# The rotary sine product on GpSimd, from a ScalarE copy of the projected query, in a two-layer attention and expert kernel

## What is computed

```python
def _apply_rope(x, sin, cos):
    return x * cos + _rotate_half(x) * sin
q_hk = (hidden_q @ Wq.T).reshape(Bv, Sv, H, K)
q_big = jnp.einsum('bshk,hkq->bshq', q_hk, w_kc_q)
q_big = _apply_rope(q_big, sin_q[None, :, None, :], cos_q[None, :, None, :])
q_r = jnp.einsum('bshq,hqr->bhsr', q_big, W_qr)
k_r = jnp.einsum('bld,hdr->bhlr', kv_r, W_kr)
scores = jnp.einsum('bhsr,bhlr->bhsl', q_r, k_r)
attn = jax.nn.softmax(scores, axis=-1)
```

## Time and profile before

| | |
|---|---|
| median of three runs | 660.13 us |
| the profiled execution, first to last instruction | 657.1 us |
| TensorE busy | 545.1 us (83%) |
| VectorE busy | 439.8 us (67%) |
| GpSimd busy | 307.2 us (47%) |
| ScalarE busy | 260.9 us (40%) |
| mean granted TensorE clock | 0.942 of full speed |
| batch 0, 1, 2, 3 begin at | about 114, 240, 371, 503 us |

### The profile page before, as it was taken

How to read it: one execution, slowest core, us unless ns; L and a number is a source line. 1 busy time by engine, 2 the same in 40 slices (tenths; PEclk the granted TensorE clock), 3 DMA queues, 4 the chain that set the end, 5 groups by cost and what they waited for, 6 DMA issues and landing times.

```text
span 657.1 us, 8656 instructions
## 1 busy us (share of the span) xinstructions
PE 545.1 (83%) x3032; PEld 341.7 (52%) x3032; DVE 439.8 (67%) x874; ACT 260.9 (40%) x706; POOL 307.2 (47%) x300
## 2 busy tenths in 40 slices
PE   2862865857898779789998897999987999999696
PEld 1851334535553457555555575555554765655442
DVE  3999893479757725997776459977774364644244
ACT  1852221243532333545345234453452165464243
POOL 3766344249628642336154442361544234445366
PEclk9986699898987799999999998999999899999798
DMA  7940100022312200000000000000000000000000
GB/s 289 399 150 6 59 0 4 1 65 96 97 33 96 88 1 21 0 5 1 1 0 1 0 17 1 1 1 1 0 2 0 17 1 1 0 2 1 17 0 16
DMA packets 10201, 24.56 MB, mean 37 GB/s; under 512 B 4464, under 2 KB 6512, under 8 KB 9264
## 3 DMA queue, kind: packets, MB, share of 16 engines
q1 hardware_dynamic: 9920, 23.24, 10.0%
q0 software_dynamic: 240, 0.79, 0.3%
HBM read 22.97 MB, written 1.05 MB: 37 GB/s over the span
## 4 chain that ended last, share of the span: by engine, by line
PE 45%; DVE 35%; ACT 7%; issue 6%; POOL 6%; DMA 0%; SPq 0%; POOLq 0%; DVEq 0%; ACTq 0%
PE s L515 9%; PE qc L515 9%; PE ga L515 9%; PE qb L515 8%; PE ua L515 6%; DVE wk L1070 4%; DVE top L1068 4%; ACT reg L865 3%; DVE reg L1154 3%; DVE amax L995 2%; PE tp L518 2%; DVE nmax L1161 2%; DVE masks L1232 2%; DVE ffn L1014 2%; DVE reg L1127 2%
## 5 line engine op out<-in xcount | busy, mean ns | idle before, releaser
L1399 POOL TENSOR_TENSOR reg<-reg,rsum 128x512 f32<-128x512 f32 x64 | 68.4, 1089 | 131.9 <-DVE rsum L1168 131.9
L865 ACT ACTIVATE reg<-s,nmax 128x256 f32<-128x256 f32 x128 | 59.0, 477 | 49.8 <-DVE nmax L1161 49.7
L1232 DVE SCALAR_TENSOR_TENSOR masks<-s,route,masks 128x256 f32<-128x256 f32 x120 | 51.4, 478 | 38.3 <-PE s L515 38.0
L515 PE MATMUL s<-wE,xhi 128*128 128x512 fp8e4 x192 | 74.4, 387 | 0.6
L515 PE MATMUL s<-wE,xlo 128*128 128x512 fp8e4 x192 | 74.2, 387 | 0.0
L515 PE MATMUL qc<-reg,wM 128*64 128x256 f32 (+1 forms) x384 | 69.6, 402 | 3.0 <-DVE reg L1154 3.0
L518 PE MATMUL tp<-idn,reg 128*128 128x128 f32 x248 | 40.4, 286 | 35.5 <-POOL reg L1399 19.0
L515 PE MATMUL qb<-reg,wA_hi 128*128 128x256 f16 x384 | 65.0, 279 | 1.5 <-ACT reg L847 1.4
L518 PEld LDWEIGHTS tp<-idn,reg 128*128 128x128 f32 x248 | 29.5, 144 | 50.7 <-POOL reg L1399 25.6
L515 PEld LDWEIGHTS qc<-reg,wM 128*64 128x64 f32 (+1 forms) x384 | 37.5, 155 | 31.9 <-issue 22.2
L783 ACT COPY reg<-tp 128x512 f32<-128x512 f32 x52 | 30.6, 588 | 56.5 <-PE tp L518 56.5
(11 more groups left out here) (194 smaller groups left out, 1118.4 us busy)
## 6 DMA issues: line engine op xcount, KB each, us to landing
masks<-in_moe_masks SPq DMA_DIRECT2D x16, 512.0 KB, 3.3
wM<-in_att_wq SPq DMA_DIRECT2D x1, 2048.0 KB, 7.9
wE<-in_wo_t SPq DMA_DIRECT2D x1, 2048.0 KB, 10.7
reg<-in_kc_q SPq DMA_DIRECT2D x1, 1536.0 KB, 11.2
reg<-in_qr_t SPq DMA_DIRECT2D x1, 1536.0 KB, 18.6
xb<-in_x SPq DMA_DIRECT2D x4, 256.0 KB, 3.4
wU<-in_gate_w SPq DMA_DIRECT2D x1, 1024.0 KB, 13.1
wD<-in_up_w SPq DMA_DIRECT2D x1, 1024.0 KB, 15.1
```

The source lines that it names most:

```text
L515: return nc.tensor.matmul(dst, lhsT, rhs, start=start, stop=stop, skip_group_check=not check)
L865: nc.scalar.activation(attn[p % 2][:, k * S:(k + 1) * S], s.tensor[:, (k % 2) * S:(k % 2 + 1) * S], ACT.Exp, bias=nmax[:, o:o + 1], accum_ ...
L1232: ins = nc.vector.scalar_tensor_tensor(acc[:, t, chain], src, w, acc[:, t, chain], ALU.mult, ALU.add)
L1399: nc.gpsimd.tensor_tensor(a, a, rsum[:, o + 2 * hh:o + 2 * hh + 2].unsqueeze(2).to_broadcast([P, 2, S]), ALU.mult).then_inc(attn_ready.sem, 1)
```

## The change

The sine product leaves VectorE. ScalarE copies the projected 128x768 tile from QB into a new SBUF tile `qcopy`, and GpSimd multiplies that by the sine table into the second half of `qcs`. VectorE keeps the cosine product, which reads QB as before, and which now also waits for the copy. `to_keys` on TensorE also waits for the sine product. The copies stand on ScalarE at these places: pair 0 after `x_turn` and ahead of the adjacency drain, pair 1 after `to_keys` of pair 0 and ahead of the tanh of the adjacency, pair p + 2 in slot p after the expert fills of the second group and ahead of `attn_turn`. The products stand on GpSimd: pair 0 as the first thing of a batch, pair 1 after `adjacency`, pair p + 2 after `attention` of slot p. For the SBUF that `qcopy` takes, the scratch space of dynamic DMAs is halved to 8192.

```diff
+        qcopy = sb("qcopy", J * S)
...
-        qc_ready = count("qc_ready", PAIRS)
+        q_copied = count("q_copied", PAIRS)
+        sin_ready = count("sin_ready", PAIRS)
...
             def to_keys(b, p):
                 pe.wait_ge(QB.drained, QB.done(("project", b, p)))
+                pe.wait_ge(sin_ready.sem, sin_ready.at(b, p + 1))
...
+            def rotate(b, p):
+
+                act.wait_ge(QB.filled, QB.done(("project", b, p)))
+                act.wait_ge(sin_ready.sem, sin_ready.at(b, p))
+                nc.scalar.copy(qcopy[:, :], QB.tensor[:, 0:J * S]).then_inc(q_copied.sem, 1)
...
                 x_turn(b)
+                rotate(b, 0)
                 if more:
                     adjacency(b + 1)
                 to_keys(b, 0)
+                rotate(b, 1)
                 if more:
                     adjacency_tanh(b + 1)
                     norm(b + 1, 0, y2, xb, y2_ready)
...
                     experts_of(experts[p][1])
+                    if p + 2 < PAIRS:
+                        rotate(b, p + 2)
                     attn_turn(b, p, 0)
...
-                for g, tab in enumerate((cosq, sinq)):
-                    nc.vector.tensor_tensor(qcs[:, g * J * S:(g + 1) * J * S], QB.tensor[:, 0:J * S], tab[:, :],
-                                            ALU.mult).then_inc(qc_ready.sem if g == 0 else QB.drained, 1)
+                dve.wait_ge(q_copied.sem, q_copied.at(b, p + 1))
+                nc.vector.tensor_tensor(qcs[:, 0:J * S], QB.tensor[:, 0:J * S], cosq[:, :], ALU.mult).then_inc(QB.drained, 1)
...
+            def rotate(b, p):
+
+                if p == 0:
+                    pool.wait_ge(ld_tab.sem, 112)
+                pool.wait_ge(q_copied.sem, q_copied.at(b, p + 1))
+                if p >= 1:
+                    pool.wait_ge(QC.filled, QC.done(("to_keys", b, p - 1)))
+                nc.gpsimd.tensor_tensor(qcs[:, J * S:2 * J * S], qcopy[:, :], sinq[:, :], ALU.mult).then_inc(sin_ready.sem, 1)
...
                 more = b + 1 < B
+                rotate(b, 0)
                 if more:
                     adjacency(b + 1)
+                rotate(b, 1)
                 if b >= 1:
                     rstd(b - 1, 3)
                 for p in range(PAIRS):
                     attention(b, p)
+                    if p + 2 < PAIRS:
+                        rotate(b, p + 2)
...
-    nc = _bacc.Bacc("TRN2", target_bir_lowering=False, num_devices=1)
+    nc = _bacc.Bacc("TRN2", target_bir_lowering=False, num_devices=1, dynamic_dma_scratch_size=8192)
```

## The result

The changed kernel takes 689.98 us, the median of four runs (687.24 to 692.93), against 659.42 us for the kernel before beside it: 4.7% more, ratio 1.0473, 95% interval 1.044 to 1.0507. The forecast was 686, with a range of 667 to 695. The profiled execution has a span of 685.4 us, 28.3 more than the 657.1 of before.

A forecast was written before the change was run, and what follows sets the result against it. TensorE, busy 83%, was taken as the bound, with VectorE time worth something only where a matmul waits for it. The terms sum to 25.7 us: span 657.1 becomes 682.8, plus 3.0 for the median, 686 us; range 667 to 695.

The forecast's parts named there:

- Term 1: Batch 0, pair 1: to_keys starts 5.4 us later behind copy, tanh and adjacency; 3.6 us plus 1.7 clock, 5.3 us.
- Term 2: Batch 0, attention of pair 1 to pair 3: two sines enter a nearly full GpSimd; 3.0 us, ends 0 and 4.5.
- Terms 3 and 4: Starts of batches 2 and 3: sine behind result and store on GpSimd delays to_keys; 5.7 and 4.6 us with clock.
- Term 5: Five slots of batches 1 to 3: copy behind ScalarE's expert fill makes VectorE late; 1.3 us x 5 = 6.5 us.
- Term 6: Slot 0 of batches 1 to 3, copy wait and disturbed subtraction; slot 5 of batches 1 and 2, late sine; 3.0 us.
- Term 7: Gain in slots 1 and 2 of batches 1 and 2, bounded by TensorE's own waits; 2.4 us won.
- Its signs: TensorE waits of some 6, 4 and 6.5 us, cosine waits over 2 us in five slots, GpSimd gapless in batch 0.
- Rival (c): Full blocking: each sine holds up VectorE's two-input instructions for its whole 1.8 us; 692 us; chance 0.13 with dearer cases.
- rival (a): Moved work pays: the chain's 10 us come in; 659 us, or 650 with TensorE slack at two batch starts; chance 0.07.

The follow-up runs named there:

- pair1_ahead: Changed kernel with the copy of pair 1 behind the adjacency tanh and its sine between the GpSimd addition and the rstd; 685.28 us, ratio 1.038.
- scratch_alone: Kernel before with only the scratch of dynamic DMAs halved; 659.08 us, ratio 0.999.
- b0_back: Changed kernel with all eight sine products of batch 0 back on VectorE; 679.65 us, ratio 1.0312.
- five_products: Changed kernel with only five of 32 sines on GpSimd and the copy ahead of the second group; 652.94 us, ratio 0.9923 to the kernel before.
- p2_back: Changed kernel with the sine product of pair 2 back on VectorE in batches 1 to 3; 689.64 us, ratio 1.047.

## Why the prediction was right, step by step

The sign, the mechanism and the size held; the sum was 25.7 us and 28.3 were measured in the trace. Part of the agreement is luck: terms 3 to 6 were short by 5.5 us together, and terms 1, 2 and 7 and the end of the kernel, which no term had, made up 3.0 of them. By its terms, each from the steps of the shift:

```
                                          predicted  measured
1  batch 0, pair 1                            5.3       5.0
2  batch 0, GpSimd full                       3.0       1.9
3  start of batch 2                           5.7       6.65
4  start of batch 3                           4.6       5.28
5  five slots, copy behind an expert fill     6.5       8.8
6  slot 0 (3.3) and slot 5 (1.3) *            3.0       4.6
7  won                                       -2.4      -2.9
   behind the last pair                        -       -1.1
                                             25.7      28.3

* slot 5's late sine is that of pair 7; it shows from pair 6 to pair 7
```

**Its signs.** The waits of TensorE are 6.30, 4.02 and 6.68 us where some 6, 4 and 6.5 were named, and the cosine waits 3.71 or 3.72 us for the copy in each of the five slots of term 5. One sign wasn't met: GpSimd isn't busy without a gap from `attention` 1 to 3, since 1.3 us stay idle, 0.87 of it in one wait for a mask.

**Prices.** 0.80 and 1.8 us were read off neighbouring shapes; 0.799 and 1.817 are measured. Taking the copy by the step from 256 to 512 columns, and the product between the two rows that bound it, was enough.

**Term 1** held as worked out: 5.18 us later, and one low-clock stretch behind it. `pair1_ahead` shows the cause. The windows view of the changed kernel, from that `to_keys` on, has the clock at 0.50, and the same after the waits of 4.02 and 6.68 us:

```profile
134.40:137.70 3.30, 3.30 (x10) 1.91 (x12) 0.18 (x1) 1.07 (x6) 1.87 (x2) 0.50 0.00 0
...
390.29:397.11 6.82, 5.50 (x20) 3.13 (x21) 0.68 (x2) 0.73 (x2) 1.22 (x1) 0.50 0.11 37
...
530.23:537.06 6.83, 4.65 (x16) 2.53 (x17) 0.00 (x0) 0.62 (x2) 2.06 (x2) 0.50 0.11 38
```

**Terms 3 and 4.** The waits were worked out at 4.0 and 4.65 us and came to 4.10 and 4.70: the order on GpSimd could be read to a tenth. What was mis-sized is the clock. In batch 2 it was put at one stretch of 3.41 us, 1.7 us lost; the stretch is 6.82 us long and costs 6.65 - 4.10 = 2.6 us, since part of it is TensorE's own wait. In batch 3, which paid some already, 0.6 us more. The bounds of term 3 (4.0 to 5.7) didn't hold the 6.65.

**Term 2** is mis-sized, or given back. The stretch is 25.11 us long with 23.83 busy, against 22.11 and 20.36 in the earlier trace rows: 3.0 us more, to the digit of the forecast. The windows view of the changed kernel:

```profile
151.82:176.93 25.11, 18.90 (x112) 12.77 (x112) 18.22 (x50) 9.95 (x29) 23.83 (x25) 0.81 0.28 91
```

But from pair 1 the shift grows by 4.07 us to pair 4, falls by 2.28 from there to pair 6, and 1.9 are left at the start of batch 1. The forecast stopped its reading at `attention` 3 and didn't ask what comes behind. What gave the time back lies at least in part in the trace of the kernel before. It has a low stretch there, which `scratch_alone`, the same streams, hasn't. Before, then `scratch_alone`:

```profile
202.59:209.41 6.82, 5.67 (x7) 2.50 (x8) 5.13 (x8) 0.60 (x1) 5.89 (x5) 0.50 0.47 154
```

```profile
202.59:209.41 6.82, 6.71 (x31) 3.87 (x32) 5.97 (x10) 1.81 (x4) 5.80 (x6) 1.00 0.47 155
```

The shift of `scratch_alone` falls by 4.4 us from pair 4 to pair 6, and that of `b0_back`, with the batch 0 of the kernel before, does so too. The changed kernel has the full clock from 183 to 212 us. So the 1.9 us measured for this term are a difference between two clock patterns as well, and its worth without them stays open.

**Term 5** was right in its five slots and short in size: 2.29, 2.22, 2.00, 1.15 and 1.15 us, not 1.3 each. The one slot that was read closely (slot 4, batch 3) is one of the two with 1.15. The other three were priced by it without a reading of their own. In slot 1 of batch 3, VectorE had 0.97 us to spare ahead of its masks, not 1.20, and hadn't waited for the bank before; its masks start 2.0 us later, and that is the cost. In slot 3 of batches 1 and 2 a second thing comes in. VectorE in batch 1, from its masks on, before:

```profile
299.30 1.74 DVE L1232 SCALAR_TENSOR_TENSOR masks<-s,route,masks 128x256 f32<-128x256 f32 x4 [1.21 <-PE s L515]
...
301.66 0.18 DVE L1000 TENSOR_SCALAR qsc<-amax 128x16 f32<-128x16 f32 x1
...
302.16 0.69 DVE L1005 TENSOR_TENSOR ffn<-ffn,qrs 128x512 f32<-128x512 f32 x1
```

and after, with GpSimd beside it:

```profile
307.08 1.65 DVE L1244 SCALAR_TENSOR_TENSOR masks<-s,route,masks 128x256 f32<-128x256 f32 x4
...
309.36 1.28 DVE L1013 TENSOR_SCALAR qsc<-amax 128x16 f32<-128x16 f32 x1
...
310.95 1.60 DVE L1018 TENSOR_TENSOR ffn<-ffn,qrs 128x512 f32<-128x512 f32 x1
...
309.33 1.27 POOL L1450 TENSOR_TENSOR masks<-masks,tern 128x512 f32<-128x512 f32 x1
310.75 1.27 POOL L1450 TENSOR_TENSOR masks<-masks 128x512 f32<-128x512 f32 x1
```

The masks are 1.31 us late beyond the shift of 6.47, as priced. From there to the row maximum VectorE takes 8.72 us in place of 7.74, and 1.31 + 0.98 are the 2.29 of the slot. Two of its quantisation steps are longer by 1.1 and 0.9 us, beside GpSimd's expert sums, which now stand behind the sine; another is shorter by 0.95. No term had this: the moved product pushes GpSimd's next instructions onto other VectorE work.

**Term 6** contains the wrong reading. The forecast took from the earlier trace rows that VectorE's two-input subtraction and a GpSimd product disturb each other "a stretch of a little over half and no more". One row more would have said otherwise. GpSimd in the kernel before, beside the instruction at 459.20:

```profile
457.21 2.85 POOL L1399 TENSOR_TENSOR reg<-reg,rsum 128x512 f32<-128x512 f32 x2 [13.43 <-DVE rsum L1168]
```

It ended at 460.06, so only 0.86 us of VectorE's 1.94 lay beside it, and 0.71 us was lost: nearly all of the overlap. The changed kernel says the same in its slot 0, VectorE and GpSimd in batches 1 and 2:

```profile
273.19 1.65 DVE L1197 TENSOR_TENSOR xlo<-masks,xhi 128x512 f16<-128x512 f32 x1
...
272.47 1.82 POOL L1413 TENSOR_TENSOR reg<-qcopy,sinq 128x768 f32<-128x768 f32 x1
...
414.24 1.70 DVE L1197 TENSOR_TENSOR xlo<-masks,xhi 128x512 f16<-128x512 f32 x1
...
413.58 1.82 POOL L1413 TENSOR_TENSOR reg<-qcopy,sinq 128x768 f32<-128x768 f32 x1
```

The sine ends at 274.29 and 415.40, 1.10 and 1.16 us after the subtraction began; its own 0.68 us on top would make 1.78 and 1.84, and 1.65 and 1.70 are measured. VectorE stood still until the sine was nearly through. The cosine ahead of it waits 1.01 us for the copy in batch 1, but VectorE has the sine's 0.95 us less to do, so it is 0.1 us late when the subtraction begins; 0.1 and the 0.97 lost in the subtraction are the 1.08 us of the slot. By the Trainium skill, SBUF — State Buffer, section "Who interferes with whom", two such instructions exclude each other for the whole instruction. This case's traces agree to within 0.15 us, by which the time lost is less than the overlap, and the forecast was wrong to set it aside. Rival (c) had the mechanism, with too high a price in slot 0: what the subtraction loses is the rest of the GpSimd instruction that is running (1.0 us here), not the whole 1.8. Of the 9.4 us by which VectorE's other instructions are longer, some 5 show in the shift, in slots 0 and 3.

The -1.1 us behind the last pair were in no term: the low stretch there is 6.82 us long, as in `five_products`, where the kernel before had 10.24. That this is the cause is argued and not shown.

**Term 7** held (-1.51 and -1.39 us, in slots 1 and 2 of batches 1 and 2): bounding the gain by TensorE's own waits was right, where the 10 us of rival (a), read off the chain, would have been wrong by a factor of three. The chain's share says how much of an engine's work lies on the path that ended last, not what the path would do without it.

**Median over span.** Put at 3.0 us, found 4.6 (689.98 - 685.4): 1.8 between the span and the time of the profiled run itself (687.24), and 2.7 because two of the runs lie 5 us above it. With the 2.6 us of the sum that is the distance from 686 to 690. The range of 667 to 695 holds all four runs.

**Not tried.** One would like the cosine not to wait for the copy. Both read all 768 columns of QB in PSUM, from two engines. By the Trainium skill, PSUM — Partial Sum Buffer, section "Terms", two engines on the same bank and quadrant at once are an error, reads included. No run here shows it, since no kernel without that wait was run. If it holds, it is what keeps the two halves of the rotation from running side by side where VectorE stood ready for QB. Nor was it tried to let the two engines read different columns at a time; QB is allocated with 1024 columns, twice the width of the other tiles in PSUM.

**Open.** Why one and the same batch 0 costs 6.9 and 7.5 us in two traces of the changed kernel and 12.7 in two kernels that differ from it only later. The low-clock stretches lie in other places from the set-up on, and sum to 3.5 us more from 113 to 257 us; what sets their places isn't shown. For the same reason term 2 has a measured size in its own stretch (3.0 us) but none in the total.

## What to carry to other kernels

Work that is moved to a half-idle engine is priced by its place in two queues, that of the engine that takes it and that of the engine that feeds it, not by its duration or by busy shares: 32 products taken off VectorE won 2.9 us, the new path cost 32 (places in queues, the low clock behind the waits, and VectorE's instructions held up beside GpSimd's), and three changes of order took 22 of them back with all products still on GpSimd. Move single instances, not the whole loop: those where the giving engine ends last, the input is there before the feeding engine arrives, and the taking engine is idle; five of 32 gave a kernel 0.8% faster than before, 0.3 to 0.4% of it by the mechanism. And read each slot that a price is used for, since three of five slots cost nearly twice what the one that was read did.

## What the runs showed that was not expected

- The same wait needn't cost the same clock: behind the same 1.98 us of wait at the start of batch 3, 12 matmuls took 3.25 us in the kernel before and 2.15 us in `five_products`.
- Batch 0 of one code ended with a shift of 6.89 and 7.54 us in two traces, and of 12.65 and 12.80 in two kernels that differ only behind it; the streams of the kernel before, traced twice, lie 1.62 us apart at the same place. A variant that is to be compared within 1% wants its stretches read one by one: from pair 0 to pair 7 the shift of `p2_back` grows by 1.31, 1.75 and 5.09 us in batches 1 to 3, against 2.57, 2.60 and 5.47 in the changed kernel, and its median shows none of these 2.5 us.
- VectorE's blocked time shows as a longer instruction, not as idle time ahead of it: 1.65 us for a subtraction of 0.68. In all, 30.3 us of products left VectorE and its busy time fell by 20.9.
